# A two-stage attention block on Trainium2: the normalised rows of the cross half made by ScalarE as scale and offset

## The reference

```python
x = x + jnp.tanh(g_xattn[0]) * xattn(_layernorm(x), ctx_1024, ctx_1024)   # cross attention, no mask
x = x + jnp.tanh(g_ffn[0]) * ffn(_layernorm(x), ...)
def _layernorm(x, axis=-1, eps=1e-05):
    m = jnp.mean(x, axis=axis, keepdims=True)
    v = jnp.var(x, axis=axis, keepdims=True)
    return (x - m) / jnp.sqrt(v + eps)
```

## Time and profile before

| | |
|---|---|
| median of 3 runs | 482.83 us (482.69 to 483.07) |
| the profiled execution, whole | 483.01 us |
| its span, first to last instruction | 480.8 us |
| TensorE, matmuls | busy 420.6 us, 87% |
| VectorE | busy 382.6 us, 80% |
| GpSimd | busy 313.5 us, 65% |
| ScalarE | busy 273.5 us, 57% |
| xp on VectorE (L597) | 32 instructions, 6.2 to 129.7 us |
| xn_all on GpSimd (L247) | 16 instructions, from 130.8 us |

### The profile page before, as it was taken

One profiled execution on the slowest core, in us unless ns is written; L12 is line 12 of the kernel. 1 busy time (PEld: TensorE's weight loads), 2 busy tenths in 40 slices (PEclk: granted clock), 3 DMA queues, 4 the chain that ended last, 5 costly groups with the idle time before them and its releaser, 6 DMA issues.

```text
span 480.8 us, 18054 instructions
## 1 busy us (share of the span) xinstructions
PE 420.6 (87%) x6804; PEld 265.6 (55%) x6804; DVE 382.6 (80%) x1205; ACT 273.5 (57%) x693; POOL 313.5 (65%) x688
## 2 busy tenths in 40 slices
PE   0378888888888999999999999997899999999983
PEld 0245454544445566666666666664467676767652
DVE  5688999999978878788877787832679899999971
ACT  1136777777676666675666666673354545454440
POOL 5465766767798888878887874220346666666654
PEclk9999999999999999999999999997699999999995
DMA  7855776755533444333344334200000000000000
GB/s 165 195 151 161 194 187 166 184 148 130 134 93 106 110 118 113 95 96 103 104 122 114 94 96 115 66 10 1 1 1 24 11 25 11 24 11 25 12 23 22
DMA packets 88022, 42.78 MB, mean 89 GB/s; under 512 B 15992, under 2 KB 87808, under 8 KB 87936
## 3 DMA queue, kind: packets, MB, share of 16 engines
q1 hardware_dynamic: 77072, 38.87, 30.6%
q10 hardware_dynamic: 10864, 2.76, 2.6%
HBM read 5.68 MB, written 2.10 MB: 16 GB/s over the span
## 4 chain that ended last, share of the span: by engine, by line
PE 37%; DVE 18%; POOL 3%; ACT 2%; issue 2%; ACTq 0%; POOLq 0%; DVEq 0%
PE u_bank L443 8%; DVE z_acc L969 5%; PE s_bank L381 5%; PE s_bank L394 4%; PE s_bank L799 2%; PE u_bank L820 2%; DVE r L617 2%; PE st_bank L799 2%; PE t_bank L373 2%; POOL z_rstd_ L697 2%; PE t_bank L367 2%; PE u_bank L456 2%; PE st_bank L394 2%; DVE z_two L945 1%; DVE z_y L994 1%
## 5 line engine op out<-in xcount | busy, mean ns | idle before, releaser
L636 DVE TENSOR_REDUCE nm<-s_bank 128x4 f32<-128x512 f32 x256 | 171.5, 682 | 37.6 <-PE s_bank L394 34.6
L526 ACT ACTIVATE pt<-st_bank 128x512 f32<-128x512 f32 x256 | 149.1, 601 | 77.2 <-PE u_bank L443 41.1
L394 PE MATMUL s_bank<-qk 64*64 64x128 bf16 (+1 forms) x1536 | 102.5, 221 | 12.2 <-DVE nm L636 7.7
L443 PE MATMUL u_bank<-pt,vaug 128*32 128x128 f32 x2048 | 109.5, 286 | 1.6 <-DVE ao L653 0.3
L394 PE MATMUL st_bank<-qk 64*64 64x128 bf16 (+1 forms) x1588 | 101.7, 218 | 0.0
L394 PEld LDWEIGHTS s_bank<-qk 64*64 64x64 bf16 (+1 forms) x1536 | 72.9, 104 | 36.1 <-issue 18.8
L394 PEld LDWEIGHTS st_bank<-qk 64*64 64x64 bf16 (+1 forms) x1588 | 72.1, 103 | 0.0
L443 PEld LDWEIGHTS u_bank<-pt,vaug 128*32 128x32 f32 x2048 | 40.8, 108 | 27.2 <-issue 3.8
L381 PE MATMUL s_bank<-mqk,idb 64*64 64x256 bf16 x256 | 38.3, 291 | 2.7 <-ACT pt L526 0.8
L884 ACT ACTIVATE z_gated<-s_bank,z_gates 128x128 f32<-128x128 f32 x64 | 18.3, 369 | 35.7 <-PE u_bank L820 35.7
L381 PE MATMUL st_bank<-mkq,idb 64*64 64x256 bf16 x256 | 38.3, 293 | 0.1
(11 more groups left out here) (121 smaller groups left out, 883.0 us busy)
## 6 DMA issues: line engine op xcount, KB each, us to landing
qk<-part SPq DMA_DIRECT2D x221, 128.0 KB, 2.8
x_all<-x SPq DMA_DIRECT2D x16, 128.0 KB, 2.8
qk<-qrow SPq DMA_DIRECT2D x32, 64.0 KB, 2.2
qk<-mts ACTq DMA_DIRECT2D x64, 32.0 KB, 2.5
out<-z_o SPq DMA_DIRECT2D x16, 128.0 KB, 1.8
c_all<-ctx_in SPq DMA_DIRECT2D x14, 128.0 KB, 3.2
ewt<-exp_t SPq DMA_DIRECT2D x1, 512.0 KB
qk<-part ACTq DMA_DIRECT2D x3, 128.0 KB, 2.7
```

Of the source, the lines that this page charges most:

```text
L394: ins = pe.matmul(to[outs, :], fixed[:, outs], moving, start=not masked, stop=True, skip_group_check=masked)
L443: ins = pe.matmul(u_bank[b][32 * j:32 * j + 32, r * P:(r + 1) * P], v, pt[m % 4][:, j, :], start=half == 0, stop=half == 1, skip_group_che ...
L526: act.activation(pt[m % 4][:, :, :].rearrange("k j q -> k (j q)"), st_bank[m % 2][:, :], ACT.Exp).then_inc(ex, 1)
L636: dve.tensor_reduce(nm[q % 2][:, first:first + HEADS], s_bank[n % 2][:, :].rearrange("q (j k) -> q j k", j=HEADS), AX_X, ALU.max, negate=T ...
```

## The change

VectorE no longer makes xp. GpSimd, right after rstd, makes for each of the two sequences of a unit offset = mean * rstd * -1, a column of 128x1; it waits for its own rstd first. ScalarE makes xp as rstd * x + offset with one ACTIVATE for each sequence (Identity, with the offset as bias and rstd as scale, each one value for a partition), at t = 0, behind the exponential of that slot. The semaphore of xp keeps its name, `ln`, and the rows of the self-attention half get one of their own, `ln1`; the waits for them are split accordingly.

```diff
@@ deviation (GpSimd) @@
                 pool.wait_ge(stat, (u + 1) * 4)
                 if u >= 2:
-                    pool.wait_ge(ln, rows_done(u - 2))
+                    pool.wait_ge(ln if in_x(u - 2) else ln1, rows_done(u - 2))
...
                 pool.tensor_tensor(rstd[u % 2][:, :], ve[u % 2][:, :], mhalf[:, :], ALU.pow).then_inc(rstd_s, 1)
+                if in_x(u):
+                    pool.wait_ge(rstd_s, u * 2 + 2)
+                    for b in range(G):
+                        pool.tensor_scalar(offset[u % 2][:, b:b + 1], mv[u % 2][:, b, 0:1], rstd[u % 2][:, b:b + 1], -1.0,
+                                           ALU.mult, ALU.mult).then_inc(off_s, 1)
@@ act_attention (ScalarE) @@
+            def normalised(u):
+                act.wait_ge(off_s, (u + 1) * G)
+                if u >= 2:
+                    act.wait_ge(tr, u - 1)
+                for b in range(G):
+                    act.activation(xp[u % 2][:, b, :].rearrange("q (x hs) -> q x hs", hs=HS),
+                                   one(x_all, u * G + b).rearrange("q (hs x) -> q x hs", hs=HS),
+                                   ACT.Identity, bias=offset[u % 2][:, b:b + 1],
+                                   scale=rstd[u % 2][:, b:b + 1]).then_inc(ln, 1)
...
                     copy_u(q)
+                if in_x(s + 2) and t == 0:
+                    normalised(s + 2)
                 if in_x(s) and t == 4:
                     values(s)
@@ dve_attention (VectorE) @@
-            def normalised(u):
-                dve.wait_ge(rstd_s, u * 2 + 2)
-                if u >= 2:
-                    dve.wait_ge(tr, u - 1)
-                for b in range(G):
-                    dve.tensor_scalar(xp[u % 2][:, b, :].rearrange("q (x hs) -> q x hs", hs=HS),
-                                      one(x_all, u * G + b).rearrange("q (hs x) -> q x hs", hs=HS),
-                                      mv[u % 2][:, b, 0:1], rstd[u % 2][:, b:b + 1],
-                                      ALU.subtract, ALU.mult).then_inc(ln, 1)
...
-                    if t == 0:
-                        normalised(s + 2)
                     if t == 3:
                         rest_of_high(s + 2)
```

More of the change, by code:

```diff
@@ L91, in gated_block_kernel @@
         ve = [sb(f"ve{i}", [P, G]) for i in range(2)]; rstd = [sb(f"rstd{i}", [P, G]) for i in range(2)]
+        offset = [sb(f"offset{i}", [P, G]) for i in range(2)]
         xp = [sb(f"xp{i}", [P, G, P]) for i in range(2)]; cp = [sb(f"cp{i}", [P, G, P]) for i in range(2)]
@@ L120, in gated_block_kernel @@
         x_in = [sem(f"x_loaded{i}") for i in range(AHEAD)]
-        stat = sem("stats"); rstd_s = sem("rstd_steps"); ln = sem("ln_applied"); ln2 = sem("ln_second_applied"); perm = sem("context_permuted")
+        stat = sem("stats"); rstd_s = sem("rstd_steps"); off_s = sem("offsets"); ln = sem("ln_applied"); ln1 = sem("ln_first_applied"); ln2 = sem("ln_second_applied"); perm = sem("context_permuted")
         rope = sem("rope_steps"); vx = sem("x_values"); vy = sem("y_values")
@@ L160, in rows_done @@
         def rows_done(u):
-            return (u + 1) * G if u < GROUPS else GROUPS * G + u - GROUPS + 1
+            return (u + 1) * G if u < GROUPS else u - GROUPS + 1
         def row(sp, dst, src, semaphore):
@@ L262, in rotate @@
                 if step == 0:
-                    pool.wait_ge(ln, rows_done(u))
+                    pool.wait_ge(ln1, rows_done(u))
                     pool.wait_ge(ln2, u - GROUPS + 1)
@@ L582, in statistics @@
                 if u >= 2:
-                    dve.wait_ge(ln, rows_done(u - 2))
+                    dve.wait_ge(ln if in_x(u - 2) else ln1, rows_done(u - 2))
                 if in_y(u - 2):
@@ L604, in first_row @@
                 dve.tensor_scalar(one(xn2_all, u * G), one(x_all, u * G), mv[u % 2][:, 0, 0:1],
-                                  rstd[u % 2][:, 0:1], ALU.subtract, ALU.mult).then_inc(ln, 1)
+                                  rstd[u % 2][:, 0:1], ALU.subtract, ALU.mult).then_inc(ln1, 1)
             def rest_of_high(u):
```

## The result

| | before | after |
|---|---|---|
| median of the runs | 482.95 us (482.69 to 483.79) | 489.48 us (488.51 to 489.88) |
| span of the profiled execution | 480.8 us | 486.7 us |
| unit of the cross half | 8.38 us | 8.75 us |

The changed kernel takes 1.0129 times as long (95% interval 1.0112 to 1.0146), 6.5 us more. The row of before has one execution more than the table ahead of the prediction. The profiled execution of after was its fastest, 488.51 us.

A forecast was written before the change was run, and what follows sets the result against it. It took rings of dependences of equal length, 8.38 us a unit, to bound the kernel, not VectorE's busy share. 3.8 + 0.8 + 1.6 + 0.6 = 6.8 us more gave 489.6 us, range 484.5 to 494.5.

The forecast's parts named there:

- Rings of equal length: Cross half: closed chains of waits through VectorE, ScalarE and GpSimd, tied at TensorE, all as long as the 8.38 us unit.
- VectorE's ring through xp: Cross half: chain from ScalarE's high part through VectorE's maxima, statistics and xp, TensorE's transposes and mts, back; 8.38 us.
- rival "faster": Cross half: VectorE is the bound and its 0.60 us is gained; 480.7 or 475 us in all, chance 0.07.
- TensorE's 0.21: TensorE's wait for xp before the input transposes, 0.21 us per unit, read as time an earlier xp would gain.
- GpSimd's term: Cross half: wait and two offsets, less mr's 0.12 and the room of 0.12, delay the transpose of the maxima 0.38 us.
- ScalarE's term: Cross half: two ACTIVATEs of 0.50 us, the pair 0.89, start the input transposes 0.18 us later (0.10 to 0.26).
- the larger delay counts and not the sum: ScalarE's 0.18 and GpSimd's 0.38 us meet at one transpose on TensorE, so each unit pays only 0.38.
- Ten steady units: Cross half, xp from 44.88 to 120.38 us: 10 x 0.38 = 3.8 us added.
- The two before: The two units ahead of the steady ones, where GpSimd has no residual: about 0.4 us each, 0.8 added.
- The last: The unit at 130 us, where TensorE already waits for GpSimd: the whole 0.62 us, counted as 0.6.
- Warm-up: First three units, where VectorE waits for rstd: 0.59 us later twice and 0.4 in the first unit, together 1.6.
- The first xp after 12 us: Warm-up sign: xp complete at 13.98 instead of 13.39 us; wrong if not about 0.6 us later.

The follow-up runs named there:

- e11: Kernel before with xp's second row on ScalarE, its offset on VectorE as a pointer tensor_scalar, and context tiles transposed first; 481.77 us, ratio 0.9972.
- e12: e7 with a spare 128x2 ACTIVATE on ScalarE ahead of each us copy, two in a unit, result unused; 484.2 us.
- e7: Kernel before with TensorE transposing the two context tiles ahead of the two xp tiles; 482.12 us, ratio 0.9972.
- e2: Kernel before with GpSimd's two offsets per unit added and not used, xp staying on VectorE; 488.71 us, ratio 1.0115.

## Why the prediction came out

**What bounds the kernel: right.** Rings of equal length, not VectorE's 95%, decided it. VectorE lost 0.60 us of queue time in a unit and the unit grew by 0.37. At least one ring was missing from the list: something through ScalarE, most likely with TensorE alone, keeps the unit at 8.37 when VectorE's ring through xp and GpSimd's are eased (e11, and the spare instruction of e12). It changed nothing here, since the change lengthens others, but by it the rival "faster" had less chance than its price of 480.7 suggested: TensorE's 0.21, on which that price stood, is in e7 a gap that is there without any wait.

**GpSimd's term: right.** Offsets took 0.264 (0.28 taken), their pair 0.50 (0.50), the residual 1.27 behind rstd (1.29), and mr gave back its 0.12. The delay by that sum is 0.36 against 0.38, and the kernels in which GpSimd alone holds the unit show 8.75 to 8.78.

**ScalarE's term: mis-sized.** The step "so one takes 0.46 to 0.54 us; I take 0.50" gave +0.18. It measured 0.618, the pair 1.11, and by the prediction's own sum 95.20 + 1.11 = 96.31 against 95.91 is +0.40. The pointer (0.09) was sized rightly, as the kernel with one pointer showed. What was left out is the permuted order of the columns, 16 elements apart, which costs 0.11 in each instruction; no row that served as a bound reads with such a step. In plain order the pair took 0.89, as in the sum:

```profile
91.02 0.89 ACT L518 ACTIVATE xp<-x_all,offset,rstd 128x128 f32<-128x128 f32 x2
```

**Hence the waits.** "TensorE waits for mst of GpSimd before the transpose of the maxima in each unit" did not come true in the steady units: both delays are equal to within 0.06 us, and the wait for xp, first in TensorE's queue, hides the other. The sign "the wait before the input transposes names ScalarE, and grows" did come, from 0.21 to 0.59. The rule that the larger delay counts and not the sum was right, and here it hid the error: 0.40 and 0.38 give nearly the same unit as 0.18 and 0.38. VectorE's share fell to 85.2%, not "under 85%", with the new waits for TensorE.

**The sum.** Ten steady units: 4.03 (3.8). That agreement is partly chance: between the ten xp from 44.88 to 120.38 lie nine distances, and these grew by 0.37 each, 3.33 together; the tenth, from the fifth unit to the sixth, grew by 0.70 (8.52 to 9.22), and why was not traced. The two before: 0.71 (0.8). The last: 0.67 (0.6). Warm-up: 2.09 (1.6), in its three units 0.57, 0.75 and 0.77 where 0.4, 0.59 and 0.59 were counted; the pair lasts 0.20 longer there than the sum had it, and lies on the path. The first xp after 12 us, before complete at 13.39, now is at 13.63 + 1.09 = 14.72:

```profile
13.63 1.09 ACT L518 ACTIVATE xp<-x_all,offset,rstd 128x128 f32<-128x128 f32 x2 [4.38 <-POOL offset L248]
```

That is 1.33 later, of which 0.57 come from the unit before it and 0.76 are its own. The prediction named "about 0.6 us later" and its absence as a sign of being wrong; by the letter this sign came true, and the cause is again the length of the pair, and the first unit's delay that the sign left out.

Together 7.5 against 6.8 at the end of the cross half. That the median came out within 0.2 us is partly luck: what follows, counted at 0, gave back 1.6 in the profiled execution (5.9 of span), and about 1.0 by the medians, which are 6.5 apart. In the profiled one part of it is the granted clock at the changeover. Of the 0.7 that the experts gave back between their first z_gated and last z_o, 0.4 lie in the last unit (z_o 471.26 to 477.88 before, 477.60 to 483.79 after). There too the clock fell earlier in before: it was 0.50 from 471 to 473 us, and 0.70 at the same place in after, 477 to 479. The other 0.3, and the 0.3 of the self-attention half, are not settled.

**The lock between VectorE and GpSimd, and the advice to offload.** The traces show each engine held by the other. VectorE's scalar_tensor_tensor with two SBUF inputs took 0.51 us beside GpSimd's copy, against 0.20 for the pointer form. VectorE's xp, a tensor_scalar, is held as well where the copy started first: the pair took 0.93 in the second unit of before and 0.88 in the steady units of e2, against 0.67, and its first row alone took 0.58 there:

```profile
90.76 0.58 DVE L603 TENSOR_SCALAR xp<-x_all,mv,rstd 128x128 f32<-128x128 f32 x1
```

That row ended 0.13 after the copy. In the steady units of before xp started first and GpSimd's mr was held: it lasted 0.34 and ended 0.1 after the first row of xp. The Trainium skill (SBUF — State Buffer, "SBUF: two separate sides") says that whichever of the two starts first has the shared ports for the whole of its instruction; these rows agree. What the prediction made of it, up to 0.67 back for GpSimd and a net of -0.05, was too much for another reason: one small instruction of GpSimd stood behind one row of xp, and 0.12 was all that it lost. The Trainium skill (Perfetto Trace Analysis, "Optimizing Scalar/DVE Operations") says that offloading to ScalarE may make sense when VectorE is saturated. Here it did not: with VectorE 95% busy in the cross half, the offload made the kernel 1.3% slower.

## What to carry to other kernels

Before work is moved off the busiest engine, measure the length of each ring of dependences through one unit, with the idle time at the place where the work would land; where several tie, work taken from one gains nothing, and work added to another beyond its idle time at that place is paid in every unit, even two instructions of one element per lane. Price a moved instruction from rows with the same access pattern as well as the same size, and test a short idle time before a weight load by looking whether it is there when nothing is waited for. Where two terms meet in a maximum, a right total does not show that the smaller was right.

## What was unexpected of the hardware

- An ACTIVATE of 128x128 f32 from SBUF to SBUF took 509 ns in plain column order and 618 ns with columns read 16 elements apart.
- A VectorE scalar_tensor_tensor of 128x1 with two SBUF inputs took 506 ns in the median beside GpSimd's work and 123 ns at its shortest; the tensor_scalar with a pointer that computes the same took 204. But a tensor_scalar of 128x128 was held by the copy too, 0.58 us in place of 0.38.
- GpSimd needs 264 ns for 128x1 with one pointer, more than ve's 193 for 128x2 without. Two of them and one wait delay the next instruction by 0.60 us.
- In the cross half of e7 the weight load of the input transposes started 0.20 us late with nothing to wait for.
- At the changeover to the experts the lower clock lasted 13.6 to 13.7 us in four of the traces and 10.2 to 10.3 in the nine others.
